# Loading a block's expert number on TensorE and VectorE without a check of its bounds

## The chip, the core and the metric

The kernel runs on one core of a Trainium2 chip. The core has five engines, each with its own instruction stream: TensorE (PE, with its weight loads shown as PEld), VectorE (DVE), ScalarE (ACT), GpSimd (POOL) and SyncE (SP). [...] Each engine has a sequencer that reads the stream, runs register instructions itself and hands the rest to the engine; in the views a "q" behind the engine's name (DVEq, PEldq) means the sequencer. The metric is the device time of one execution in microseconds.

## What is computed

A batch of 16 images of 128 channels and 16 x 16 pixels goes through a convolution block with filters made from the data, then self attention over the pixels of pairs of images, then a layer of eight experts, each token going to its best two. Only the last part matters here:

```python
scores = xf @ router_w + router_b
topk_p, topk_i = jax.lax.top_k(jax.nn.softmax(scores, axis=-1), K)        # K = 2 of E = 8
gates = jnp.zeros((T, E), xf.dtype).at[jnp.arange(T)[:, None], topk_i].set(topk_p)
h = jnp.einsum('td,edh->teh', xf, w1) + b1[None]
gated = jax.nn.silu(jnp.einsum('teh,ehf->tef', h, wg) + bg[None]) * (jnp.einsum('teh,ehf->tef', h, wv) + bv[None])
y = jnp.einsum('tef,efd->ted', gated, w2) + b2[None]
out = jnp.einsum('ted,te->td', y, gates)
```

There are 4096 tokens, so 8192 pairs of token and expert. They are sorted by expert into rows in memory and worked off in 71 blocks of 128 rows, each block of one expert.

## The kernel before

The first 205 us are the convolution, the attention, the routing and the preparation of the experts' weights; the change touches none of them. Behind them stands a loop over the 71 blocks, written out block by block, in which each engine has a fixed order.

Which expert a block belongs to is known only at run time. A table of two halves holds, for each block, its first row and its expert (`table`, one partition, int32). The first half covers the first 41 blocks and is made before the loop; the second half is computed by DVE inside the loop, in five pieces behind blocks 4, 6, 8, 10 and 12 (`second_table`), and copied in behind block 16.

For block j the work goes as follows. SP loads the row number from the table and starts the transfer of the block's rows into a ring of 14 buffers (line 1516). PE transposes the rows (line 1722). ACT makes the high part (line 1537) and DVE the low part (line 1659) of the transposed block. PE multiplies the high part with the high and the low half of the expert's weights (lines 1727, 1728) and the low part with the high half (line 1736). ACT applies silu (line 1549), and DVE multiplies with the other half and the token's weight (line 1684). PE transposes the result (line 1745), ACT copies it (line 1541), and PE multiplies with the expert's second weights (line 1756). DVE scales the expert's bias and adds it (line 1668, `scale`), and POOL scatters the block's result to memory (line 1461).

PE and DVE pick the expert's slice of the weights and the bias by a number in a register of their sequencer. PE loads it in `expert_of(j)` (line 1715), one block ahead, between the high and the low products. DVE loads it at the head of `scale(j)` (line 1664), right behind line 1684 of block j + 2. Both loads declare the bounds 0 and 7.

DVE's order in one turn of the loop is: low part of block j + 1, line 1684 of block j, `scale` of block j - 2, and then, in some turns, a piece of the second table. From turn 59 on a sum of results follows instead (lines 1673 and 1677), one a turn for twelve turns. These sums read results back from memory; their first transfer starts when the scatters of the first 55 blocks have landed. PE's order in one turn is: transpose of block j + 1, the high products of j, the load of the number of j + 1, the low product of j, the transposes of j - 1, the down product of j - 2. What follows the loop is the scatter of the last blocks, the last transfers back, four sums and the store.

Of the kernel before, what the change touches and what calls it, by code (L numbers as in the profile page):

```python
# [1365 lines left out]
def expert_programs(sb, sem, out, g):  # L1366
# [6 lines left out]
    E, NB, U = EXPERTS, BLOCKS, RING  # L1373
# [30 lines left out]
    table = sb("table", [1, 2, 2, P], I32)  # L1404
# [29 lines left out]
    def half_of(j):  # L1434
        return int(j >= A)

    def entry(j):
        return j - A * half_of(j)
# [212 lines left out]
    def vector(dve, second_list):  # L1651

        dve.wait_ge(g["ld_b2"], 16)
        dve.wait_ge(S["table_ready"], 1)

        def low_part(j):

            dve.wait_ge(S["xhigh_done"], j + 1)
            dve.tensor_tensor(x_low[:, j % 2, :], bank_x[j % 2][:, 0:P], x_high[:, j % 2, :], ALU.subtract).then_inc(S["xlow_done"], 1)  # L1659

        def scale(j):

            u = j % U
            e = dve.value_load(table[0:1, half_of(j), 1, entry(j):entry(j) + 1], min_val=0, max_val=E - 1)
            dve.wait_ge(S["y_psum"], j + 1)
            if j >= U:
                dve.wait_ge(ys_sent[u], 16 * (j // U))
            dve.scalar_tensor_tensor(ys[:, u, :], b2_all[:, bass.ds(e * C, C)], xs[:, u, C:C + 1], bank_y[j % 2][:, 0:C],  # L1668
                                     ALU.mult, ALU.add).then_inc(S["ys_done"], 1)

        def first_sum(p):
            dve.wait_ge(y_loaded[p], 16 * 2)
            dve.tensor_tensor(t2[:, p, :, :], t2[:, p, :, :], y_first[:, p, :, :], ALU.add).then_inc(S["sum1_done"], 1)

        def second_sum(p):
            dve.wait_ge(S["sum1_done"], p + 1)
            dve.tensor_tensor(y_second[p], t2[:, p, :, :], y_second[p], ALU.add).then_inc(S["sum_done"], 1)

        low_part(0)
        for j in range(NB):  # L1680
            if j < NB - 1:
                low_part(j + 1)
            dve.wait_ge(S["silu_done"], j + 1)
            dve.scalar_tensor_tensor(gated[:, j % 2, :], bank_h[j % 2][:, HID:2 * HID], xs[:, j % U, C:C + 1], silu[:, j % 2, :],  # L1684
                                     ALU.mult, ALU.mult).then_inc(S["gated_done"], 1)
            if j >= 2:
                scale(j - 2)
            second_list(j)
            p, k = divmod(j - max(NB - 2 * SPLIT - 4, EARLY + 4), 2)
            if 0 <= p < SPLIT:  # L1690
                if k == 0:
                    first_sum(p)
                else:
                    second_sum(p)
        scale(NB - 2)
        scale(NB - 1)
        for p in range(SPLIT, PAIRS - 1):
            first_sum(p)
            second_sum(p)

        p = PAIRS - 1
        dve.wait_ge(y_loaded[p], 16 * 2)
        for h in range(2):
            dve.tensor_tensor(t2[:, p, 2 * h:2 * h + 2, :], t2[:, p, 2 * h:2 * h + 2, :], y_first[:, p, 2 * h:2 * h + 2, :], ALU.add).then_inc(S["sum1_done"], 1)
            dve.wait_ge(S["sum1_done"], PAIRS + h)
            into = y_second[p][:, 2 * h:2 * h + 2, :]
            dve.tensor_tensor(into, t2[:, p, 2 * h:2 * h + 2, :], into, ALU.add).then_inc(S["sum_done"], 1)

    def tensor(pe, second_list):
        pe.wait_ge(g["wlow_done"], E)  # L1710
        pe.wait_ge(g["ld_w2"], 16)
        pe.wait_ge(S["table_ready"], 1)

        def expert_of(j):
            return pe.value_load(table[0:1, half_of(j), 1, entry(j):entry(j) + 1], min_val=0, max_val=E - 1)

        def x_transpose(j):
            if j == 0:
                pe.wait_ge(g["rank_free"], PAIRS - 1)
                pe.wait_ge(g["gt_free"], 4 * PAIRS)  # L1720
            pe.wait_ge(xs_loaded[j % U], 16 * (j // U + 1))
            pe.transpose(bank_x[j % 2][:, 0:P], xs[:, j % U, 0:C], ident).then_inc(S["xt_psum"], 1)  # L1722

        def hidden_high(j, e):

            pe.wait_ge(S["xhigh_done"], j + 1)
            pe.matmul(bank_h[j % 2][:, :], x_high[:, j % 2, :], w_high[:, bass.ds(e * (2 * HID), 2 * HID)], start=True, stop=False)  # L1727
            pe.matmul(bank_h[j % 2][:, :], x_high[:, j % 2, :], w_low[:, bass.ds(e * (2 * HID), 2 * HID)], start=False, stop=False)  # L1728

        def hidden_low(j, e):  # L1730
            if j == 0:

                for _ in range(2):
                    pe.matmul(bank_h[1][:, 0:2 * P], ident, ident_mean, start=True, stop=True)
            pe.wait_ge(S["xlow_done"], j + 1)
            pe.matmul(bank_h[j % 2][:, :], x_low[:, j % 2, :], w_high[:, bass.ds(e * (2 * HID), 2 * HID)], start=False, stop=True).then_inc(S["h_psum"], 1)  # L1736

        def gated_transpose(j):
            if j == 0:
                pe.wait_ge(g["image_free"], PAIRS)  # L1740
            pe.wait_ge(S["gated_done"], j + 1)
            if j > 0:
                pe.wait_ge(S["gt_done"], j)
            for h in range(2):
                last = pe.transpose(bank_g[:, h * P:(h + 1) * P], gated[:, j % 2, h * P:(h + 1) * P], ident)  # L1745
            last.then_inc(S["gt_psum"], 1)

        def down(j, e):

            if j == 0:  # L1750
                pe.wait_ge(g["attn_free"], PAIRS)
            pe.wait_ge(S["gt_done"], j + 1)
            if j >= 2:
                pe.wait_ge(S["ys_done"], j - 1)
            for h in range(2):
                last = pe.matmul(bank_y[j % 2][:, 0:C], gatedt[:, j % 2, h * P:(h + 1) * P], w2_all[:, bass.ds(e * (2 * C) + h * C, C)],  # L1756
                                 start=(h == 0), stop=(h == 1))
            last.then_inc(S["y_psum"], 1)

        known = {0: expert_of(0)}  # L1760
        x_transpose(0)
        for j in range(NB):
            if j < NB - 1:
                x_transpose(j + 1)
            hidden_high(j, known[j])
            if j < NB - 1:
                known[j + 1] = expert_of(j + 1)
            hidden_low(j, known[j])
            if j > 0:
                gated_transpose(j - 1)  # L1770
            if j > 1:
                down(j - 2, known[j - 2])
            second_list(j)
        gated_transpose(NB - 1)
        down(NB - 2, known[NB - 2])
        down(NB - 1, known[NB - 1])
# [49 lines left out]
```

## Time and profile before

| | us |
|---|---|
| median of 3 runs | 339.78 |
| lowest and highest of them | 339.06, 340.17 |
| the profiled execution | 338.92 |
| its span, first to last instruction | 336.8 |
| PE busy, share of the span | 295.7, 88% |
| DVE busy | 232.7, 69% |
| POOL busy | 164.2, 49% |
| ACT busy | 144.5, 43% |
| mean granted TensorE clock, share of full speed | 0.958 |

Busy time counts what an engine itself executes. Register instructions, waits and issues of the sequencers are not in it; they show as idle time of the engine before its next instruction. The chain that ended last is followed back from the last instruction, at each step to what released it; its "issue" is time in which the engine waited for nothing that the profile shows.

### The profile page before, as it was taken

To read this page: it belongs to the slowest core of one execution; us is meant where nothing else is said; L and a number is where in the kernel's file an instruction comes from. 1 tells how busy PE (TensorE), PEld (TensorE's weight loads), DVE (VectorE), ACT (ScalarE), POOL (GpSimd) and SP (SyncE) were. 2 spreads that over 40 slices of the span, in tenths; PEclk is the share of its full clock that TensorE was granted. 3 is DMA by queue.
4 is the path that set the end of the run, shared out by engine and by line. 5 is a ranking of instruction groups with operands and counts; after the bars stand their busy time and mean duration, and the time that the engine had idled before them with its cause. 6 is when DMAs were issued, how large, how long until landed. Compare 5 with 4: busy or idle time off the path is not lost.

```text
span 336.8 us, 7115 instructions
## 1 busy us (share of the span) xinstructions
PE 295.7 (88%) x1721; PEld 237.2 (70%) x1721; DVE 232.7 (69%) x1012; ACT 144.5 (43%) x464; POOL 164.2 (49%) x187
## 2 busy tenths in 40 slices
PE   2989999999999999999977756999999999988930
PEld 2757787777877778777856644778888888867720
DVE  2344365679697887968887885687766667648943
ACT  0444333536244362533212223555666666654510
POOL 4000002021264647656847847477777777563550
PEclk9999999999999999999988985999999999997985
DMA  6742332140213600100101114333333333249625
GB/s 191 282 156 75 99 106 69 51 123 0 78 56 98 227 19 32 34 25 26 48 25 41 42 49 107 97 105 107 101 92 90 104 106 104 80 132 299 223 79 187
DMA packets 29920, 33.39 MB, mean 99 GB/s; under 512 B 5064, under 2 KB 23836, under 8 KB 29626
## 3 DMA queue, kind: packets, MB, share of 16 engines
q1 hardware_dynamic: 24608, 23.64, 23.8%
q0 software_dynamic: 4352, 8.60, 7.4%
q10 hardware_dynamic: 922, 0.71, 0.6%
q8 instruction: 16, 0.26, 0.3%
q14 instruction: 22, 0.18, 0.2%
HBM read 21.69 MB, written 11.68 MB: 99 GB/s over the span
## 4 chain that ended last, share of the span: by engine, by line
PE 68%; DVE 17%; DMA 5%; issue 4%; ACT 3%; DVEq 1%; POOL 1%; SPq 0%; POOLq 0%; ACTq 0%
PE bank L1157 9%; PE bank L1756 7%; PE bank L1074 6%; PE bank L1167 4%; PE bank L1142 4%; PE bank L1736 4%; PE bank L1149 4%; PE bank L1727 4%; PE bank L1745 3%; PE bank L1728 3%; PE bank L1069 3%; PE bank L1111 2%; DVE ys L1668 2%; PE bank L1089 2%; PE bank L1722 2%
## 5 line engine op out<-in xcount | busy, mean ns | idle before, releaser
L1461 POOL DMA_INDIRECT moe_dram<-ys,xs x71 | 69.6, 980 | 35.6 <-issue 19.5
L429 POOL DMA_INDIRECT rows_dram<-row,slot x56 | 55.6, 993 | 24.9 <-issue 13.5
L1756 PE MATMUL bank<-w_all,gatedt 128*128 x284 | 44.4, 280 | 0.1
L1549 ACT ACTIVATE silu<-bank 128x256 f32<-128x256 f32 x71 | 27.2, 383 | 38.8 <-PE bank L1736 38.8
L1684 DVE SCALAR_TENSOR_TENSOR gated<-bank,xs,silu 128x256 f32<-128x256 f32 x71 | 34.2, 481 | 9.1 <-ACT silu L1549 5.3
L1668 DVE SCALAR_TENSOR_TENSOR ys<-b_all,xs,bank 128x128 f32<-128x128 f32 x71 | 24.7, 347 | 21.3 <-issue 19.6
L1756 PEld LDWEIGHTS bank<-w_all,gatedt 128*128 128x128 f32 x284 | 38.0, 195 | 0.3 <-issue 0.3
L1727 PE MATMUL bank<-w_high,x_high 128*128 x71 | 34.5, 486 | 0.2 <-ACT x_high L1537 0.2
L1736 PE MATMUL bank<-w_high,x_low 128*128 x71 | 29.8, 420 | 3.4 <-DVE x_low L1659 2.9
L1157 PE MATMUL bank<-zhat,const 121*128 121x256 f32 (+1 forms) x128 | 31.1, 398 | 1.1 <-DVE zhat L714 1.1
L440 POOL TENSOR_TENSOR frstd<-fvar,minus_half 128x2 f32<-128x2 f32 x7 | 4.9, 706 | 51.5 <-DVE fvar L801 51.5
L1745 PE MATMUL bank<-const,gated 128*128 128x128 f32 x142 | 27.8, 278 | 0.8 <-DVE gated L1684 0.8
L1728 PE MATMUL bank<-w_low,x_high 128*128 x71 | 28.4, 401 | 0.0
L1157 PEld LDWEIGHTS bank<-zhat,const 121*128 121x128 f32 (+1 forms) x128 | 24.8, 199 | 4.7 <-issue 1.1
L1541 ACT ACTIVATE gatedt<-bank 128x256 f32<-128x256 f32 x71 | 26.9, 379 | 1.4 <-PE bank L1745 1.4
L1745 PEld LDWEIGHTS bank<-const,gated 128*128 128x128 f32 x142 | 19.2, 141 | 9.9 <-DVE gated L1684 2.3
L1537 ACT ACTIVATE x_high<-bank 128x128 fp32r<-128x128 f32 x71 | 19.6, 277 | 9.9 <-PE bank L1722 3.1
L1074 PE MATMUL bank<-gt,const 128*121 128x256 f32 (+1 forms) x96 | 22.8, 385 | 0.0
L1736 PEld LDWEIGHTS bank<-w_high,x_low 128*128 128x128 f32 x71 | 13.6, 191 | 12.4 <-DVE x_low L1659 7.1
L446 POOL TENSOR_TENSOR gn_rstd<-gn_var,minus_half 128x2 f32<-128x2 f32 x8 | 5.7, 714 | 33.0 <-DVE gn_var L962 33.0
L1659 DVE TENSOR_TENSOR x_low<-bank,x_high 128x128 fp32r<-128x128 f32 x71 | 20.1, 284 | 0.9 <-ACT x_high L1537 0.7
L1722 PE MATMUL bank<-const,xs 128*128 128x128 f32 x71 | 19.6, 279 | 0.8 <-DVE pos L773 0.8
(204 smaller groups left out, 622.4 us busy)
## 6 DMA issues: line engine op xcount, KB each, us to landing
xs<-rows_dram SPq DMA_DIRECT2D x71, 66.0 KB, 1.9
xc<-in_x SPq DMA_DIRECT2D x8, 256.0 KB, 2.8
wgv<-in_wg SPq DMA_DIRECT2D x8, 256.0 KB, 2.8
wgv<-in_wv SPq DMA_DIRECT2D x8, 256.0 KB, 3.1
xt<-in_xt SPq DMA_DIRECT2D x4, 512.0 KB, 4.5
xt<-moe_dram SPq DMA_DIRECT2D x8, 256.0 KB, 3.5
moe_dram<-ys,xs POOLq DMA_INDIRECT x71, 2.3
const<-in_const SPq DMA_DIRECT2D x1, 1123.0 KB, 9.2
```

What stands on the lines that cost most here:

```text
L429: pool.indirect_dma_start(rows_dram, bass.IndirectOffsetOnAxis(ap=slot[:, f % 2, 2 * t + k:2 * t + k + 1], axis=0), row[:, f % 2, t, k, :] ...
L1074: last = pe.matmul(bank_s[r // 2][0:tile_rows[r], r % 2 * 2 * C:(r % 2 + 1) * 2 * C], fwd[:, h, tile_cols[r]], gt[:, b % 2, h, :], start=( ...
L1157: last = pe.matmul(bank_o[:, h * 2 * C:(h + 1) * 2 * C], inv[0:tile_rows[r], r, h * P:(h + 1) * P], zhat[0:tile_rows[r], r, :], start=(r = ...
L1461: pool.indirect_dma_start(moe_dram, bass.IndirectOffsetOnAxis(ap=xs[:, u, C + 1:C + 2].bitcast(U32), axis=0), ys[:, u, :], None, bounds_ch ...
L1549: act.activation(silu[:, j % 2, :], bank_h[j % 2][:, 0:HID], ACT.Silu).then_inc(S["silu_done"], 1)
L1668: dve.scalar_tensor_tensor(ys[:, u, :], b2_all[:, bass.ds(e * C, C)], xs[:, u, C:C + 1], bank_y[j % 2][:, 0:C], ALU.mult, ALU.add).then_in ...
L1684: dve.scalar_tensor_tensor(gated[:, j % 2, :], bank_h[j % 2][:, HID:2 * HID], xs[:, j % U, C:C + 1], silu[:, j % 2, :], ALU.mult, ALU.mult ...
L1727: pe.matmul(bank_h[j % 2][:, :], x_high[:, j % 2, :], w_high[:, bass.ds(e * (2 * HID), 2 * HID)], start=True, stop=False)
L1728: pe.matmul(bank_h[j % 2][:, :], x_high[:, j % 2, :], w_low[:, bass.ds(e * (2 * HID), 2 * HID)], start=False, stop=False)
L1736: pe.matmul(bank_h[j % 2][:, :], x_low[:, j % 2, :], w_high[:, bass.ds(e * (2 * HID), 2 * HID)], start=False, stop=True).then_inc(S["h_psu ...
L1745: last = pe.transpose(bank_g[:, h * P:(h + 1) * P], gated[:, j % 2, h * P:(h + 1) * P], ident)
L1756: last = pe.matmul(bank_y[j % 2][:, 0:C], gatedt[:, j % 2, h * P:(h + 1) * P], w2_all[:, bass.ds(e * (2 * C) + h * C, C)], start=(h == 0), ...
```

## The change

Two calls lose their bounds; nothing else is touched. SP's load of the row number (line 1513) keeps its own.

```diff
@@ -1661,7 +1661,7 @@
         def scale(j):
 
             u = j % U
-            e = dve.value_load(table[0:1, half_of(j), 1, entry(j):entry(j) + 1], min_val=0, max_val=E - 1)
+            e = dve.value_load(table[0:1, half_of(j), 1, entry(j):entry(j) + 1])
             dve.wait_ge(S["y_psum"], j + 1)
             if j >= U:
                 dve.wait_ge(ys_sent[u], 16 * (j // U))
@@ -1712,7 +1712,7 @@
         pe.wait_ge(S["table_ready"], 1)
 
         def expert_of(j):
-            return pe.value_load(table[0:1, half_of(j), 1, entry(j):entry(j) + 1], min_val=0, max_val=E - 1)
+            return pe.value_load(table[0:1, half_of(j), 1, entry(j):entry(j) + 1])
 
         def x_transpose(j):
             if j == 0:
```

The table's expert numbers are held to at most 7 where the table is made (lines 1592 and 1633).

## Rows read from the trace of the kernel before

**Rows 1.** The page: its head, and the chain that ended last by engine.
```profile
span 336.8 us, 7115 instructions
...
PE 68%; DVE 17%; DMA 5%; issue 4%; ACT 3%; DVEq 1%; POOL 1%; SPq 0%; POOLq 0%; ACTq 0%
```

**Rows 2.** Busy time by stretch: length, engines (instructions), granted clock, DMA share, GB/s.
```profile
205.00:217.00 12.00, 10.77 (x55) 8.21 (x56) 6.07 (x23) 5.84 (x20) 6.68 (x7) 0.82 0.40 104
217.00:236.00 19.00, 18.45 (x115) 13.98 (x114) 15.43 (x57) 10.57 (x34) 13.76 (x15) 1.00 0.37 106
236.00:299.00 63.00, 63.00 (x429) 54.79 (x428) 43.79 (x128) 39.89 (x129) 46.36 (x48) 1.00 0.34 96
...
309.00:324.00 15.00, 13.72 (x87) 10.71 (x85) 13.35 (x35) 7.45 (x23) 8.74 (x9) 1.00 0.62 210
```

**Rows 3.** Instructions of lines 1664, 1715, 1668: ns least/median/most, first and last start.
```profile
L1664 DVEq TENSOR_LOAD <-table x71: 298/307/823, 212.6 to 323.0; - x71
L1664 DVEq FUSED_REGOPS  x71: 190/190/206, 213.2 to 323.4; - x71
L1664 DVEq SEQ_ASSERT  x71: 23/23/35, 213.5 to 323.6; - x71
...
L1715 PEldq FUSED_REGOPS  x71: 151/151/165, 205.3 to 318.5; - x71
L1715 PEldq SEQ_ASSERT  x71: 18/18/24, 205.5 to 318.7; - x71
...
L1668 DVEq FUSED_REGOPS  x71: 57/57/65, 213.5 to 323.7; - x71
```

**Rows 4.** DVE's instructions in time, 240 us: start, duration, [idle before <-releaser].
```profile
240.44 0.48 DVE L1684 SCALAR_TENSOR_TENSOR gated<-bank,xs,silu 128x256 f32<-128x256 f32 x1
241.25 0.35 DVE L1668 SCALAR_TENSOR_TENSOR ys<-b_all,xs,bank 128x128 f32<-128x128 f32 x1 [0.34 <-issue]
```

**Rows 5.** DVE by line, 236 to 299 us: busy, mean ns | idle before.
```profile
L1668 DVE SCALAR_TENSOR_TENSOR ys<-b_all,xs,bank 128x128 f32<-128x128 f32 x42 | 14.6, 348 | 15.0 <-issue 15.0
```

**Rows 6.** The chain that ended last, 216 to 224 us: start, duration, what.
```profile
219.14 0.43 DVE gated L1684
...
219.61 0.19 DVEq L1664
...
219.84 0.02 DVEq L1664
...
219.91 0.06 DVEq L1668
...
220.01 0.35 DVE ys L1668
...
221.38 0.29 DVE x_low L1659
```

**Rows 7.** Waits, 217 to 236 us: us in total, times, longest.
```profile
PEld bank L1736 <- DVE x_low L1659: 2.3, 4, 0.8
```

**Rows 8.** The chain that ended last, 204 to 207 us.
```profile
205.14 0.11 DVE pos L773
205.25 0.46 issue
205.71 0.46 PE bank L1722
```

**Rows 9.** DVE's instructions in time, 299 to 306 us.
```profile
303.22 0.69 DVE L1673 TENSOR_TENSOR t<-t,xt 128x512 f32<-128x512 f32 x1 [2.72 <-DMA wgv<-moe_dram]
```

**Rows 10.** DVE by line, 309 to 323 us.
```profile
L1668 DVE SCALAR_TENSOR_TENSOR ys<-b_all,xs,bank 128x128 f32<-128x128 f32 x10 | 3.5, 347 | 1.5 <-issue 0.8 <-PE bank L1756 0.3
```

**Rows 11.** PE's instructions in time, 313 to 315 us.
```profile
314.02 0.49 PE L1736 MATMUL bank<-w_high,x_low 128*128 x1 [0.29 <-issue]
```

**Rows 12.** POOL's instructions in time, 278 to 299 us.
```profile
282.26 0.98 POOL L1461 DMA_INDIRECT moe_dram<-ys,xs  x1 [0.30 <-issue]
...
290.92 0.97 POOL L1461 DMA_INDIRECT moe_dram<-ys,xs  x1 [1.78 <-DVE ys L1668]
...
297.33 0.98 POOL L1461 DMA_INDIRECT moe_dram<-ys,xs  x1 [0.30 <-issue]
```

## The prediction

> **What bounds the kernel now.** I read the head of the page first [rows 1]: 336.8 us from first to last instruction, TensorE (PE) carrying 68% of the chain that ended last and VectorE (DVE) 17%; 1% of the chain is DVE's sequencer, which is where a check of bounds is executed. All touched code runs in the expert part, so the next view was the busy time by stretch from 205 us on [rows 2]. The reader should see three different stages. From 236 to 299 us PE is busy for 63.00 of 63.00 us at the full granted clock of 1.00: 42 blocks [rows 5] in 63 us, 1.50 us each, and nothing that DVE saves can shorten that. From 217 to 236 us PE is not full, and DVE is at 15.43 of 19 us; from 309 to 324 us DVE is at 13.35 of 15 us and PE at 13.72. In these two DVE has extra work (the second block table, then the result sums), and the chain runs through it.
>
> The third view is the list of instructions by source line [rows 3]. A bounded load is three sequencer instructions: the load itself (307 ns median on DVE), a fused register operation (190 ns on DVE, 151 on PE) that compares, and an assertion (23 and 18 ns). The address arithmetic of the bias slice stands apart, on line 1668, with 57 ns, so it should stay.
>
> **The change part by part.** It removes two of those three instructions, 71 times on each of the two engines. It adds no wait, moves no instruction past another and leaves SP's own bounded load of the row number alone, so no queue gets a different order.
>
> *What one removal is worth on DVE.* In the full stretch line 1684 ends at 240.44 + 0.48 = 240.92 and line 1668 starts at 241.25 [rows 4]; 42 such gaps make 15.0 us [rows 5]. In the gap stand the rest of the load, the comparison, the assertion and the address. The chain of waits prints them one by one at 219 us [rows 6]: line 1684 ends at 219.57, the comparison starts at 219.61, the assertion at 219.84, the address at 219.91, line 1668 at 220.01. Without the check the address can stand where the comparison stood: 219.91 - 219.61 = 0.30 us earlier. The floor for one removal is the busy time of the two instructions, 0.21 us; the ceiling is the whole gap, 0.36.
>
> *217 to 236 us.* In every second block DVE builds a piece of the second table behind line 1668, and the low part of the next block (line 1659, 221.38 in rows 6) waits behind that piece. PE's third product, line 1736, waits for this low part four times, 2.3 us in all [rows 7]. So there the 0.30 us travels: earlier scale, earlier table piece, earlier low part, earlier PE. The pattern of rows 6 stands on the chain four times in full (the first comparison at 216.06, the last at 229.69). Between two of them the other block's removal is lost, because line 1684 then waits for the activation. Four times 0.30 = 1.2 us; each wait of PE is 2.3 / 4 = 0.58 us on average, so the saving fits inside. Bounds: four times 0.21 = 0.8, and four times 0.36 = 1.4.
>
> *The first load on PE.* The chain goes from the positions on DVE through 0.46 us of issue to the first transpose at 205.71 [rows 8]. In that 0.46 lie the first comparison and assertion (151 + 18 ns and the sequencer's gaps); I take 0.30 as on DVE. [...]
>
> *PE's other 70 loads.* I cost them at about 0.1 in all. The cover is PE's own work: its sequencer runs ahead of products that take 1.50 us a block, and only after a stop has it no lead. If that cover were gone, each would cost up to 151 + 18 ns.
>
> *236 to 299 us.* Zero from the products, but line 1668 comes 0.30 earlier against PE in each block, and one such block matters: the first result sum (line 1673) waits 2.72 us for a transfer [rows 9] that needs the results of the first 55 blocks in memory. The last of them starts 0.30 earlier: 0.3 us. Floor 0.
>
> *309 to 324 us.* DVE has a sum of some 0.69 us behind every scale. Its ten scales have 1.5 us of idle time before them [rows 10], of which 0.3 us is put down to PE. On PE line 1736 stands 0.29 us without a releaser at 314.02 [rows 11], right behind a slow load. If DVE gave back all it could, PE would be next: 15 us hold 13.72 of its work. I take 1.0; floor 0.4 (PE's busy share catches the rest), ceiling 1.5.
>
> Sum: 1.2 + 0.3 + 0.1 + 0.3 + 1.0 = 2.9 us. The profiled execution took 338.92 us, 2.1 more than its span and 0.86 less than the median of the three runs, 339.78. Against its own time the sum gives 336.0; I forecast the median: 339.78 - 2.9 = 336.9.
>
> **The rivals.**
>
> *The scatter on POOL holds the end.* POOL sends each block's result out. At 282.26 us it starts 0.30 us after its previous one ended, that is, back to back, has a pause of 1.78 us before 290.92 and is back to back again at 297.33 [rows 12]. It is this queue that the transfer of rows 9 waits for. If POOL can't start earlier by what DVE and PE gained (its pause could stay at its time), then DVE only waits longer at line 1673, 2.72 + 1.9 = 4.6 us, and only the 1.0 us after it is left: 338.8. Against it: POOL's backlog begins with the early blocks, and these come earlier too.
>
> *The check is covered.* The gaps of rows 4 to 6 speak against it: if the load and its check ran while line 1684 waits for the activation, line 1668 would follow with no gap, and there are 42 gaps of 0.36 us. Then nothing changes: 339.8, within 0.3%. [...]
>
> *Slower: the bounds are paid at the uses.* An expert number of unknown range could make each slice that it selects carry a check. DVE has one use a block, so it would gain nothing; PE has four (lines 1727, 1728 and twice 1756), so 4 x 0.17 - 0.17 = 0.51 us more a block for its sequencer. That decides as soon as the sequencer's block is longer than the 1.50 us of the products; a block that is already filled would cost up to 71 x 0.51 = 36 us: 376 us. Against it: lines 1513 and 1516 on SP have the same form, and line 1668 shows address arithmetic alone. It is also the case in which the change doesn't do what it says.
>
> **How the numbers follow.** The forecast has 0.68, POOL 0.15, the covered check 0.12, the slower case 0.05. The forecast's own bounds are 0.8 + 0 + 0 + 0 + 0.4 = 1.2 and 1.4 + 0.5 + 0.1 + 0.3 + 1.5 = 3.8 us: 336.0 to 338.6. Medians of three runs spread by some 0.5 us, and the POOL case at 338.8 belongs inside: 335.4 to 339.1, with the covered check and the slower case left out. A measurement of this kernel can tell about 0.3%, 1.0 us, from no change. Faster by more than that is nearly all of the forecast and half of the POOL case, 0.74; within it the other half and the covered check, 0.20; slower 0.06.
>
> **What would show it.** Right: lines 1664 and 1715 have the load alone; the gap before line 1668 in the full stretch falls from 0.36 to about 0.06 us, while 42 blocks still take 63 us; line 1736 waits for the low part some 1.2 us less between 217 and 236 us; the wait at line 1673 stays near 2.7 us; the ten scales of the last stretch lose most of their 1.5 us. Wrong: line 1673 waits 1.5 us or more longer (POOL), the gap before line 1668 stays (covered, or paid at the uses), or new register operations show on lines 1727 and 1756.

## The result, and the profile after

The changed kernel takes 384.15 us (median of 4 runs, 383.35 to 385.60) against 339.98 us of the kernel before beside it. The ratio is 1.128, 95% interval 1.124 to 1.133. The forecast was 336.9 us with a range to 339.1; what came is the third rival, the bounds are paid at the uses. The ratios and intervals here and below are of fast runs alone: one of no_check's ten runs, of 1644.57 us, and three of before_half's ten, of 341.5 to 343.6 us, count in the medians and not in the ratios.

The page of the profiled execution after the change: its head, busy time, and the chain that ended last by engine.

```profile
span 383.8 us, 7541 instructions
...
PE 343.2 (89%) x1721; PEld 247.6 (65%) x1721; DVE 233.9 (61%) x1012; ACT 144.1 (38%) x464; POOL 164.1 (43%) x187
...
PE 78%; DVE 9%; DMA 5%; issue 4%; ACT 3%; POOL 0%; SPq 0%; DVEq 0%; POOLq 0%; ACTq 0%
```

The span is 47.0 us longer than that of [rows 1]. The instruction count does not fall by 4 a block, as a removal on both engines would make it, but rises by 7541 - 7115 = 426, 6 for each of the 71 blocks. PE's share of the chain goes from 68% to 78%.

Where the new instructions stand is seen in the list by source line (ns least/median/most, first and last start; PEldq and DVEq are the sequencers of PE and DVE).

```profile
L1664 DVEq TENSOR_LOAD <-table x71: 298/304/790, 216.0 to 370.3; - x71
...
L1668 DVEq FUSED_REGOPS  x142: 46/132/234, 216.6 to 371.2; - x142
L1668 DVEq SEQ_ASSERT  x71: 23/23/35, 216.9 to 371.2; - x71
...
L1715 PEldq TENSOR_LOAD <-table x71: 297/302/712, 207.6 to 364.3; - x71
...
L1727 PEldq FUSED_REGOPS  x142: 37/108/186, 209.0 to 366.3; - x142
L1727 PEldq SEQ_ASSERT  x71: 18/18/24, 209.3 to 366.2; - x71
...
L1728 PEldq SEQ_ASSERT  x71: 18/18/18, 209.5 to 366.4; - x71
...
L1736 PEldq SEQ_ASSERT  x71: 18/18/18, 210.1 to 366.6; - x71
...
L1756 PEldq FUSED_REGOPS  x284: 37/105/174, 215.2 to 370.2; - x142
L1756 PEldq SEQ_ASSERT  x142: 18/18/18, 215.5 to 370.2; - x142
```

Lines 1664 and 1715 have the load alone now, 304 and 302 ns, against [rows 3]. But the assertions stand where the number is used. DVE's 71, of 23 ns each, are four lines further on, on line 1668 and not on 1664. PE had 71, all on line 1715; now it has 355 of 18 ns, five a block: 71 each on lines 1727, 1728 and 1736 and 142 on line 1756. Three of the five (1727 and both on 1756) also bring a long fused register operation of up to 174 to 186 ns beside a short one of 37 ns. In the kernel before each of these three uses had one fused operation of 46 ns and no assertion.

The full stretch of [rows 2] after the change (length, busy time of PE, PEld, DVE, ACT, POOL with instructions, granted clock, DMA share, GB/s), and two rows by line of the same stretch (busy, mean ns | idle before, and what ended it):

```profile
236.00:299.00 63.00, 62.92 (x288) 40.72 (x287) 30.46 (x94) 26.59 (x86) 33.90 (x35) 1.00 0.24 68
```

```profile
L1668 DVE SCALAR_TENSOR_TENSOR ys<-b_all,xs,bank 128x128 f32<-128x128 f32 x29 | 10.1, 348 | 17.0 <-PE bank L1756 16.6 <-issue 0.3
...
L1736 PEld LDWEIGHTS bank<-w_high,x_low 128*128 128x128 f32 x28 | 5.2, 187 | 8.5 <-issue 8.5
```

PE still looks full, 62.92 of 63 us at the full clock, but it holds 288 product records where [rows 2] has 429, and 29 blocks where [rows 5] has 42. Line 1668 has stopped waiting for its own sequencer (15.0 us of issue in [rows 5]) and waits for PE. And PE's weight loads show idle time put down to issue. The clock has no part in it: it is 1.00 in both.

The chain that ended last shows the same block from both sides: start, duration, what. First the kernel before, at 270 us, then the changed kernel.

```profile
270.64 0.27 PE bank L1736
270.92 0.22 PE bank L1745 x2
271.13 0.45 PE bank L1756 x4
271.58 0.11 PE bank L1722
271.69 0.23 PE bank L1727
```

```profile
270.47 0.42 PE bank L1736
270.89 0.22 PE bank L1745 x2
271.11 0.03 issue
271.14 0.91 PE bank L1756 x4
272.05 0.11 PE bank L1722
272.16 0.33 PE bank L1727
```

The lines without an expert number, 1745 and 1722, keep their 0.22 and 0.11 us. Those with it are stretched: line 1756 from 0.45 to 0.91 us, line 1736 from 0.27 to 0.42, line 1727 from 0.23 to 0.33. The chain names PE's products; the cause is in the records of PE's sequencer between them (start, duration, instruction, line; PE's own products and weight loads are left out):

```
270.740  173 ns  FUSED_REGOPS L1756
270.972   18 ns  SEQ_ASSERT   L1756
271.049   37 ns  FUSED_REGOPS L1756
271.164  173 ns  FUSED_REGOPS L1756
271.395   18 ns  SEQ_ASSERT   L1756
271.472   37 ns  FUSED_REGOPS L1756
271.587  173 ns  FUSED_REGOPS L1727
271.819   18 ns  SEQ_ASSERT   L1727
271.895   37 ns  FUSED_REGOPS L1727
```

One checked use follows the other at 271.164 - 270.740 = 0.424 us. In the kernel before the same two uses stand at 270.674 and 270.799, 0.125 us apart, with one 46 ns operation each. So a checked use costs PE's sequencer 0.30 us more: 173 + 18 + 37 - 46 = 182 ns of work, and two more gaps between instructions of 59 ns each (270.913 to 270.972, 270.990 to 271.049). No run here shows what fills the gaps of 59 ns.

For one block that makes 3 x 0.30 for the full checks, 2 x (0.018 + 0.059) = 0.15 for the bare assertions on lines 1728 and 1736, less some 0.32 for the check that left the load (measured at the first load, in the part on the prediction): 0.73 us more. The measured pace, from the start of line 1736 in block 16 to that in block 60, went from 64.81 to 97.36 us, that is from 1.473 to 2.213 us a block: 0.74 more. The two agree better than they should, since the sequencer's own pace before was 1.44 to 1.45 us (the cut kernels of the last experiment): by the sum it comes to 2.17 to 2.18, some 0.04 short of what was measured. Over all 71 blocks, from the first transpose on PE to the last scale on DVE, 118.14 us became 163.11. This is 45.0 of the 47.0 us of span; the blocks also began 2.5 us later (208.22 against 205.71), within the 205.5 to 208.6 us at which they begin in the runs below.

That the sequencer has fallen behind shows in one more place. In the kernel before, its load of the expert number (line 1715) starts 0.45 us before PE's weight load of line 1728 in the same turn (median of blocks 16 to 60); in the changed kernel it starts 0.05 us after it.

### The profile page after: what moved, and what is told of

It is laid out like the page before. It is cut to its first block, busy times and chain, and to the rows that moved or that the text cites. A ratio compares the mean times of both kernels' runs of the same rounds, so it can differ in the third digit from the quotient of the medians.

```text
span 383.8 us, 7541 instructions
## 1 busy us (share of the span) xinstructions
PE 343.2 (89%) x1721; PEld 247.6 (65%) x1721; DVE 233.9 (61%) x1012; ACT 144.1 (38%) x464; POOL 164.1 (43%) x187
## 4 chain that ended last, share of the span: by engine, by line
PE 78%; DVE 9%; DMA 5%; issue 4%; ACT 3%; POOL 0%; SPq 0%; DVEq 0%; POOLq 0%; ACTq 0%
PE bank L1756 15%; PE bank L1157 8%; PE bank L1736 8%; PE bank L1727 6%; PE bank L1074 6%; PE bank L1728 4%; PE bank L1167 4%; PE bank L1745 4%; PE bank L1142 4%; PE bank L1149 3%; PE bank L1069 3%; PE bank L1111 2%; PE bank L1722 2%; PE bank L1089 2%; DMA small<-in_small 1%
## 5 line engine op out<-in xcount | busy, mean ns | idle before, releaser
L1756 PE MATMUL bank<-w_all,gatedt 128*128 x284 | 65.0, 324 | 0.8 <-issue 0.2
L1756 PEld LDWEIGHTS bank<-w_all,gatedt 128*128 128x128 f32 x284 | 42.3, 188 | 23.4 <-issue 15.6
L1736 PE MATMUL bank<-w_high,x_low 128*128 x71 | 35.5, 501 | 1.2 <-issue 0.5
L1727 PE MATMUL bank<-w_high,x_high 128*128 x71 | 35.4, 499 | 0.6 <-ACT x_high L1537 0.6
```

## The experiments

The table gives, for each kernel, the median, the ratio to before on the same chip, and from its trace the length of four pieces of the expert part. Each kernel has one trace, so the pieces are of one execution each. The pieces go by the start of line 1736's product in blocks 4, 16, 60 and 62, and of line 1668's scale in block 68; the column "a block" is the pace in the full stretch, (16 to 60) / 44.

| kernel | median us | ratio [95%] | 4 to 16 | 16 to 60 | a block | 60 to 62 | 62 to scale 68 |
|---|---|---|---|---|---|---|---|
| before | 339.98 | 1 | 20.42 | 64.81 | 1.473 | 6.86 | 15.15 |
| after | 384.15 | 1.128 [1.124, 1.133] | 26.62 | 97.36 | 2.213 | 5.04 | 20.33 |
| pe_only | 384.31 | 1.127 [1.120, 1.133] | 26.62 | 97.26 | 2.210 | 4.46 | 20.12 |
| dve_only | 340.87 | 0.998 [0.995, 1.001] | 20.28 | 64.77 | 1.472 | 6.89 | 15.43 |
| after_half | 384.96 | 1.127 [1.120, 1.134] | 26.57 | 97.38 | 2.213 | 4.88 | 20.23 |
| no_check | 337.70 | 0.990 [0.986, 0.994] | 19.04 | 64.63 | 1.469 | 5.74 | 14.16 |
| no_check_again | 338.67 | 0.992 [0.989, 0.996] | 18.91 | 64.63 | 1.469 | 7.23 | 14.00 |
| one_use | 341.37 | 1.003 [1.000, 1.006] | 20.09 | 66.23 | 1.505 | 6.92 | 14.71 |
| two_uses | 354.45 | 1.043 [1.038, 1.048] | 21.84 | 76.60 | 1.741 | 5.01 | 16.18 |
| skip_dve | 335.92 | 0.991 [0.988, 0.994] | 19.05 | 64.70 | 1.470 | 5.82 | 14.06 |
| skip_pe | 338.47 | 0.998 [0.996, 1.001] | 19.99 | 64.61 | 1.468 | 5.91 | 14.68 |
| before_half | 340.24 | 0.997 [0.993, 1.001] | 20.15 | 63.78 | 1.450 | 7.28 | 15.70 |
| no_check_half | 335.63 | 0.989 [0.985, 0.993] | 18.65 | 60.93 | 1.385 | 9.61 | 14.41 |
| skip_dve_half | 337.58 | 0.991 [0.988, 0.995] | 19.08 | 63.20 | 1.436 | 7.64 | 14.91 |

### Which engine pays

**pe_only**: the kernel before with PE's edit alone.

```diff
@@ line 1715
-            return pe.value_load(table[0:1, half_of(j), 1, entry(j):entry(j) + 1], min_val=0, max_val=E - 1)
+            return pe.value_load(table[0:1, half_of(j), 1, entry(j):entry(j) + 1])
```

> Only PE's load has no bounds; DVE's load keeps its own. Sequencer theory (an expert number of unknown range is checked at each of PE's five uses, and PE's sequencer then needs about 2.2 us a block where the products need 1.50): 384 us, within 2 of the changed kernel. Rival (the cost sits on DVE, whose check now stands behind the wait for PE's down product): within 2 us of the kernel before, 340.

**dve_only**: the kernel before with DVE's edit alone.

```diff
@@ line 1664
-            e = dve.value_load(table[0:1, half_of(j), 1, entry(j):entry(j) + 1], min_val=0, max_val=E - 1)
+            e = dve.value_load(table[0:1, half_of(j), 1, entry(j):entry(j) + 1])
```

> Only DVE's load has no bounds; PE's load keeps its own. Sequencer theory: PE's stream is that of the kernel before, DVE has one use a block and so pays the check once, as before: 339 to 341 us. Rival (the cost sits on DVE): 384 us.

Measured: pe_only 384.31 us, the whole of the loss; dve_only 340.87, ratio 0.998 with 1 in its interval. DVE by line from 236 to 299 us in dve_only:

```profile
L1668 DVE SCALAR_TENSOR_TENSOR ys<-b_all,xs,bank 128x128 f32<-128x128 f32 x42 | 14.6, 347 | 15.7 <-issue 15.7
```

The 15.0 us of [rows 5] are 15.7: DVE has one use a block, so its 71 assertions of 23 ns only moved from line 1664 to line 1668, behind the same load and in front of the same scale. Every one of the 44 us belongs to PE.

### Is it the sequencer, or the products that look busy?

**after_half**: the changed kernel with line 1728's product on half its columns.

```diff
@@ line 1728
-            pe.matmul(bank_h[j % 2][:, :], x_high[:, j % 2, :], w_low[:, bass.ds(e * (2 * HID), 2 * HID)], start=False, stop=False)
+            pe.matmul(bank_h[j % 2][:, 0:HID], x_high[:, j % 2, :], w_low[:, bass.ds(e * (2 * HID), 2 * HID)][:, 0:HID], start=False, stop=False)
```

> The changed kernel, with PE's second product (line 1728) over half of its columns, so a quarter of the hidden layer's low weights is left out; the sequencer's instructions stay the same. 256 columns fewer are about 0.12 us of PE a block, 8 us over 71 blocks. Sequencer theory: the products have some 0.7 us of room a block, so 384 us, within 1.5. Rival (the products themselves became slower and set the pace): 376 us.

Measured: 384.96 us, no change. (Half of the product is left out, not the quarter that the expectation names.) PE by line, 236 to 299 us, in after_half:

```profile
L1736 PE MATMUL bank<-w_high,x_low 128*128 x29 | 14.4, 496 | 1.6 <-issue 0.2
...
L1728 PE MATMUL bank<-w_low,x_high 128*128 x29 | 8.1, 278 | 0.0
```

The cut product fell to 278 ns from the 396 of the changed kernel's page, and the pace stayed at 2.213 us a block. Products that can be cut for nothing do not set the pace, although PE's busy time says they fill the stretch.

### Is the cost in proportion, or does it begin at a threshold?

**one_use** and **two_uses** start from no_check (below), which has no check on either engine. They give PE a second name for the number, without declared bounds, and use it at one or at both of the weight slices on line 1756. The edit is cut to the lines that matter; "..." stands for what is left out.

```diff
@@ line 1715
-            return nc.values_load(..., engines=(mybir.EngineType.PE,), min_val=0, max_val=E - 1, skip_runtime_bounds_check_because="...")
+            free = nc.values_load(..., engines=(mybir.EngineType.PE,))
+            return free, nc.s_assert_within(free, 0, E - 1, skip_runtime_bounds_check_because="...")
@@ line 1756, one_use
-                ... w2_all[:, bass.ds(e * (2 * C) + h * C, C)],
+                ... w2_all[:, bass.ds((free if h else e) * (2 * C) + h * C, C)],
@@ line 1756, two_uses
+                ... w2_all[:, bass.ds(free * (2 * C) + h * C, C)],
```

> no_check, and of PE's five uses of the expert number one alone, the second of the two weight slices on line 1756, takes the value without declared bounds, so that 71 checks come back on PE. Theory (PE's sequencer sets the pace only where its work for a block is longer than the products'): the sequencer needs about 1.11 us for a block of no_check and 0.30 more for one checked use, 1.41 us, still under the 1.47 us of the products; so the time stays that of no_check within 1.5 us, 336 to 340. Rival (every checked use costs the path the same, wherever it stands): the 44 us of the changed kernel over five checked uses are about 9 us each, so 346 us.

> As one_use, but both weight slices on line 1756 take the value without declared bounds: 142 checks on PE. Theory: the sequencer needs 1.11 + 0.60 = 1.71 us for a block against 1.47 us of products, 0.24 us more, on about 62 blocks 15 us: 348 to 356 us, and the step from one checked use to two is far larger than that from none to one. Rival (each use the same): 355 us, with one_use at 346, a step as large as the first.

Measured: 341.37 us with one checked use and 354.45 with two, against 338.67 without (no_check_again, on the same chip). The added checks by source line (the edit makes line 1756 line 1760), first one_use, then two_uses:

```profile
L1760 PEldq FUSED_REGOPS  x213: 42/46/213, 211.8 to 323.9; - x107
L1760 PEldq SEQ_ASSERT  x71: 18/18/24, 212.2 to 323.9; - x71
```

```profile
L1760 PEldq FUSED_REGOPS  x284: 37/108/186, 212.5 to 337.4; - x142
L1760 PEldq SEQ_ASSERT  x142: 18/18/24, 212.8 to 337.3; - x142
```

The same 71 checks cost 2.7 us the first time and 13.1 us the second: there is a threshold, and the rival of equal prices (346, then 355) falls at its first step. But my own step was off too. I had the sequencer at 1.41 us a block with one checked use and so no cost; the pace rose from 1.469 to 1.505 us and the time by 2.7 us, to 1.4 us above the range that I had written. The sums of the expectations, 1.71 and 1.41 us a block, are 0.03 us short of the measured pace with two uses and 0.1 with one, so the threshold is reached earlier than the sum says. From one use to two the pace rises by 0.236, and from there to the changed kernel, with one more full check and two bare assertions, by 0.472 us.

### What a check that is really gone gives

**no_check**: both numbers are loaded with the same bounds declared and trusted, so that no check is made at the load or at the use (the edit also hands `nc` to the function around them).

```diff
@@ line 1664
-            e = dve.value_load(table[0:1, half_of(j), 1, entry(j):entry(j) + 1], min_val=0, max_val=E - 1)
+            e = nc.values_load(table[0:1, half_of(j), 1, entry(j):entry(j) + 1], engines=(mybir.EngineType.DVE,), min_val=0, max_val=E - 1, skip_runtime_bounds_check_because="...")
@@ line 1715
-            return pe.value_load(table[0:1, half_of(j), 1, entry(j):entry(j) + 1], min_val=0, max_val=E - 1)
+            return nc.values_load(table[0:1, half_of(j), 1, entry(j):entry(j) + 1], engines=(mybir.EngineType.PE,), min_val=0, max_val=E - 1, skip_runtime_bounds_check_because="...")
```

> Both loads declare the bounds 0 and 7, but no check is made of them, neither at the load nor at the uses. Sequencer theory: PE's sequencer needs about 0.3 us a block less than before, the products set the pace again, and the gains that the prediction summed for a removed check show: 336.9 us (335.9 to 338.6); DVE's gap ahead of line 1668 in the full stretch falls from 0.36 to about 0.06 us. Rival (the check of the kernel before is covered everywhere): 340 us. Rival (the loss has nothing to do with checks): 384 us.

**no_check_again**: the same kernel.

> The same kernel as no_check, beside the three that follow it, on one chip: neither the loads nor the uses of the expert number are checked on PE or DVE. It came out at 0.990 of before, about 3.4 us less. My theory (the check that is really gone gives what the sum of the prediction made, 2.9 us): 336 to 338.5 us, ratio 0.986 to 0.995. Rival (the 3.4 us were a chance of that run, since its blocks began 2 us later in the profiled execution and still ended sooner): within 0.3% of before, 339 to 342.

Measured: 337.70 us (0.990) and 338.67 us (0.992), 2.7 to 3.4 us below before by the ratios, where the sum of the prediction made 2.9. The profile of no_check: its head, then DVE by line from 236 to 299 us.

```profile
span 335.1 us, 6831 instructions
```

```profile
L1684 DVE SCALAR_TENSOR_TENSOR gated<-bank,xs,silu 128x256 f32<-128x256 f32 x43 | 20.8, 483 | 15.0 <-ACT silu L1549 14.6 <-issue 0.4
L1668 DVE SCALAR_TENSOR_TENSOR ys<-b_all,xs,bank 128x128 f32<-128x128 f32 x43 | 14.9, 347 | 3.4 <-issue 1.1
```

The 284 instructions are gone (7115 - 6831 = 4 x 71), and the list by source line shows which: both loads stand alone, and the address of line 1668 is as in [rows 3].

```profile
L1664 DVEq TENSOR_LOAD <-table x71: 299/306/1251, 214.6 to 321.5; - x71
...
L1668 DVEq FUSED_REGOPS  x71: 57/57/65, 215.2 to 322.1; - x71
...
L1715 PEldq TENSOR_LOAD <-table x71: 295/304/933, 207.0 to 316.8; - x71
```

So the fused operation and the assertion behind each load in [rows 3], 190 + 23 ns on DVE and 151 + 18 ns on PE, are the check of the bounds, as the prediction had read them. (PE's load itself has a median of 302 ns in the kernel before.) The gap in front of line 1668 fell from 15.0 us in [rows 5] to 3.4, 0.08 us each. The idle time turned up in front of line 1684, which waits for the activation; in the kernel before this line had, in the same window,

```profile
L1684 DVE SCALAR_TENSOR_TENSOR gated<-bank,xs,silu 128x256 f32<-128x256 f32 x43 | 20.8, 483 | 3.8 <-ACT silu L1549 0.2
```

So 11.6 us went from the one and 11.2 came to the other: in the full stretch DVE gains nothing.

**skip_dve** and **skip_pe** take one engine's check away and leave the other's as before: the first of no_check's two edits alone, and the second alone.

> DVE's expert number is loaded with its bounds taken on trust, so no check at the load or the use; PE's load keeps its check as before. Where do the 2.7 to 3.4 us of no_check come from? Theory of the sum (DVE's check holds the low halves for four blocks, 1.2 us, and the result sums at the end, 1.0 us): most of the gain is DVE's: 337.5 to 339, ratio 0.991 to 0.996, and skip_pe gives 0.7 us at most. Rival (it is PE's sequencer, as one_use, which has no check on DVE and one on PE, came out no faster than before): within 0.3% of before here, and the gain with skip_pe.

> PE's expert number is loaded with its bounds taken on trust, so no check at the load or the five uses; DVE's load keeps its check as before. Theory of the sum (PE's terms were 0.3 and 0.1 us): 0.7 us at most, ratio 0.997 to 1.000. Rival (PE's sequencer): the gain of no_check, 2.7 to 3.4 us, ratio 0.990 to 0.994.

Measured: skip_dve 335.92 us, 0.991 [0.988, 0.994]; skip_pe 338.47, 0.998 [0.996, 1.001]. The time of skip_dve is 1.6 us under the range that I had written, its ratio at the edge of it. The gain is DVE's, as the sum had it, and the rival that took it from PE's sequencer falls. Line 1668 in skip_pe, 236 to 299 us:

```profile
L1668 DVE SCALAR_TENSOR_TENSOR ys<-b_all,xs,bank 128x128 f32<-128x128 f32 x43 | 15.0, 348 | 15.0 <-issue 15.0
```

That is [rows 5] again, with DVE's check in place.

### Do the products set the pace before?

**before_half**, **no_check_half** and **skip_dve_half**: after_half's edit of line 1728, in the kernel before, in no_check and in skip_dve.

> The kernel before, with line 1728's product on half of its columns: half of the term with the low weights is left out. In the changed kernel the same cut changed nothing. Theory: in the kernel before the products set the pace (1.47 us a block) with the sequencer close behind (about 1.41 us); the cut takes some 0.12 us from the products of a block, of which the sequencer lets 0.06 through, on 44 to 62 blocks 3 to 4 us: 335 to 338 us. Rival (products alone set the pace): 0.12 on 62 blocks, 7 us or more: 333 or less. Rival (the sequencer already sets the pace before): no change, 339 to 341.

> no_check with line 1728's product on half of its columns: half of the term with the low weights is left out. In the kernel before this cut gave 1 us or less. Theory (there the sequencer, at about 1.41 us for a block, stood right behind the products): without the checks the sequencer needs 1.11 us, so the 0.12 us of a block come through on 44 to 62 blocks, 5 to 7 us below no_check: 331 to 334. Rival (something else holds the blocks at their pace, the chain x_low, silu, gated or POOL's scatters): 1 us or less, 337 to 339.

> skip_dve with line 1728's product on half of its columns: half of the term with the low weights is left out. DVE is unchecked, PE's load keeps its check. The cut brought the pace of the full stretch (start of line 1736 from block 16 to 60, over 44) from 1.473 to 1.450 us a block with both checks, and to 1.385 without them. Theory (PE's sequencer, with the check of its load, stands behind the products): the pace stays near 1.45 here. Rival (it is DVE, whose scale waits for its own check): 1.385 to 1.40, as without checks. The time itself tells little by either, 334.5 to 338 us, as the first result sum waits for POOL's scatters.

Measured: 340.24 us (0.997 [0.993, 1.001]), 335.63 (0.989 [0.985, 0.993]) and 337.58 (0.991 [0.988, 0.995]). No one of the three can be told from its own kernel without the cut. For the first two my theory had forecast 3 to 7 us, and missed.

The traces say why. The cut is worth 1.469 - 1.385 = 0.084 us a block, as no_check_half shows. In before_half only 1.473 - 1.450 = 0.023 of it came through, and in skip_dve_half, where PE's check stays and DVE's is gone, 1.470 - 1.436 = 0.034. So it is PE's sequencer with its one check that stands right behind the products before the change, at 1.44 to 1.45 us a block; between the two runs DVE's check makes 0.014. A run with the cut and DVE's check alone was not made, and these are paces of one trace each. The weight loads of line 1736 have the sign of it, 236 to 292 us, in skip_dve_half and then in no_check_half:

```profile
L1736 PEld LDWEIGHTS bank<-w_high,x_low 128*128 128x128 f32 x39 | 7.3, 187 | 4.9 <-issue 1.7
```

```profile
L1736 PEld LDWEIGHTS bank<-w_high,x_low 128*128 128x128 f32 x40 | 7.5, 188 | 1.9 <-issue 0.2
```

In no_check_half the 44 blocks are 3.7 us shorter than in no_check, but blocks 60 to 62 are 2.4 to 3.9 us longer than in the two runs of no_check. There the first result sum waits. DVE, and POOL's scatters up to that of block 54, the last of the three (start, duration, [idle before <-releaser]):

```profile
301.07 0.69 DVE L1673 TENSOR_TENSOR t<-t,xt 128x512 f32<-128x512 f32 x1 [5.55 <-DMA wgv<-moe_dram]
```

```profile
292.53 0.98 POOL L1461 DMA_INDIRECT moe_dram<-ys,xs  x1 [0.30 <-issue]
293.81 0.98 POOL L1461 DMA_INDIRECT moe_dram<-ys,xs  x1 [0.30 <-issue]
295.09 0.98 POOL L1461 DMA_INDIRECT moe_dram<-ys,xs  x1 [0.30 <-issue]
```

The wait of line 1673 grew from 2.72 us in [rows 9] to 5.55, and POOL's scatters stand back to back, one every 1.28 us. The scatter of block 54, the last that the transfer behind this wait needs, starts 3.64 us after the end of its scale here, 1.26 in no_check and 1.14 before: POOL is that much behind. This is the POOL rival of the prediction, met at a faster pace than the removal of the checks brings. In no_check the same wait is

```profile
303.45 0.69 DVE L1673 TENSOR_TENSOR t<-t,xt 128x512 f32<-128x512 f32 x1 [2.80 <-DMA wgv<-moe_dram]
```

so there POOL took next to nothing back (in no_check_again the wait is 3.07 us, and the scatter of block 54 starts 1.26 us after its scale as well).

## Why the prediction was wrong

**The step that failed** is the first of the change part by part: it removes two of the three instructions, and adds no wait. It removes them at the load and puts them at each use: PE has five assertions a block in place of one, its sequencer some 0.73 us more work a block, and the blocks go at 2.213 us instead of 1.473. The prediction rested this on the address arithmetic of line 1668 standing apart with 57 ns, and on SP's lines of the same form. Both belong to loads with bounds: the kernel before has 71 assertions on each of the load lines 1513, 1664 and 1715 and none on lines 1516, 1668, 1727, 1728, 1736 and 1756, where the numbers are used. They say nothing of a number that has no bounds. Among the rows there was none of an unbounded number used as an index, and the rival that followed from this should have had a chance to match, not 0.05.

**The slower rival** had the mechanism, the place and the threshold. Its size came from four uses at 0.17 us less 0.17: 0.51 us a block, 36 us. There are five assertions, since line 1736 uses the number too; a full check costs 0.30 and not 0.17, since its recorded work is 182 ns more and two gaps of 59 ns between sequencer instructions count too; and the check removed from the load was worth 0.32, not 0.17. Three full checks and two bare assertions of 0.077 us, less that, make 0.73 us a block where the rival had 0.51; the loop became 45.0 us longer where it had 36. Its price should have been taken as the prediction took DVE's, by the distance of starts and not by durations.

**The terms of the sum** hold for a change that does remove the check, as far as they can be told apart. None of them came with the change itself.

- 217 to 236 us: forecast 1.2. Blocks 4 to 16 became 1.37 us shorter in skip_dve, 0.43 in skip_pe, 1.38 and 1.51 in no_check. The place is right too: PE waits for the low half in blocks 6, 8, 10 and 14 in all of these runs, 2.3 us before [rows 7], 2.1 in skip_pe, 1.1 in skip_dve, and in no_check

```profile
PEld bank L1736 <- DVE x_low L1659: 1.2, 4, 0.4
```

- The first load on PE: forecast 0.30. The issue piece of [rows 8], 0.46 us, is in the chain of no_check

```profile
207.44 0.11 DVE pos L773
207.55 0.14 issue
207.68 0.46 PE bank L1722
```

  It is 0.32 us shorter. The changed kernel has this gain at the load as well (0.13 us of issue there), and pays it back at the first use: from the end of the positions (line 773) to the start of the first high product (line 1727) is 1.35 us before, 1.35 in the changed kernel and 1.04 in no_check. The bounds of this term in the sum, 0 and 0.5 us, are shown by no run; what the traces have is the 0.46 us of issue before, and the 0.32 that came off it.
- PE's other loads: forecast 0.1. skip_pe as a whole has 0.998 [0.996, 1.001], 0.6 us, which holds the first load's 0.3 and cannot tell the rest from nothing. But the lead that the prediction gave PE's sequencer was small: 1.44 to 1.45 us against 1.47 a block (the prediction's 1.50 is 63 us over the 42 scales seen in them).
- The first result sum: forecast 0.3. Not settled: blocks 60 to 62 took 5.74 us in no_check and 7.23 in no_check_again, the same kernel, with 6.86 before.
- 309 to 324 us: forecast 1.0. From block 62 to the scale of block 68 it is 0.99 and 1.15 us shorter in no_check and no_check_again, 1.09 in skip_dve, 0.47 in skip_pe (dve_only, which changes nothing there, is 0.28 longer, so this is the scatter). The size is right, but the row that I named as its sign is not: ten scales from 309 to 323 us still have 1.5 us of idle time in no_check, as in [rows 10]. That window holds earlier blocks there, whose loop began 2 us later; over the scales of blocks 60 to 69 the idle time goes from 1.46 us to 1.08 and 1.11, not the loss of most of it that I had named.

**The check is covered**: no. The gap in front of line 1668 closes from 15.0 to 3.4 us when DVE's check goes. And the load of the number does not run ahead of a DVE instruction that waits for another engine: in no_check DVE is idle for more than 0.25 us before line 1684 44 times, all but one put down to the activation, and each time the load behind it starts 12 to 14 ns after line 1684 itself has started. Where line 1684 only stands behind DVE's own work, the load starts up to 0.80 us before it. So the load did not run while line 1684 waited for the activation, which this rival needed.

**What the prediction said would show it** was good enough to find the cause: new register operations on lines 1727 and 1756.

## What to carry to other kernels

In these kernels the bounds declared at the load of the expert number stand for one check a block on each engine, 71 assertions on line 1715 and 71 on line 1664, and none at the uses. Without them every use has its own: 355 assertions on PE, five a block, and 71 on DVE, one a block. So count the uses on each engine before a bound is dropped, price a check by the distance between starts (0.30 us here, of which 0.18 us is recorded work), and where the range is known by construction, declare the bounds as trusted: that is the version that is faster than both, 0.990 to 0.992 of before, and DVE's edit alone, 0.991, gives all that can be measured of it. Compare the sequencer's pace for one block with that of the products too: here they were 1.44 to 1.45 and 1.47 us with the check at PE's load, and on no_check one checked use lengthened the block by 0.036 us, two by 0.272.

## What the runs showed that I had not expected

- A PE that is busy for 62.92 of 63 us can be waiting for its sequencer: the recorded lengths of its products grew instead (line 1756: a mean of 324 ns on the page of after, 280 before). The signs are fewer products in the same busy time, idle time put down to issue on the weight loads, and products that can be cut without effect.
- The chain that ended last gave PE's sequencer no share at all in the changed kernel, though it sets the pace for 71 blocks. The list by source line shows its instructions.
- The same check costs PE nothing that can be measured at the load (skip_dve at 0.991 against no_check at 0.990 and 0.992) and some 2.7 us at a use (one_use), with a recorded work of 151 + 18 = 169 ns at the load and 208 + 18 + 42 - 46 = 222 ns at the use. Why the place matters was not tried. On PE the load does run ahead in the kernel before, by 0.45 us of line 1728's weight load, while in one_use the weight load behind the check starts 0.05 us after the check's last operation ended (median of blocks 16 to 60).
